# Vision transformer attention: weighted values in two groups a turn, and row maxima of five slots in two halves

## The chip, the cores and the metric

One core of one Trainium2 chip runs the whole program. The metric is the device time of one execution in microseconds (us). The kernel before was run three times: 3645.43, 3633.97 and 3636.25 us, median 3636.25 us.

## The reference

A four-layer vision transformer (64 images, 197 tokens, 8 heads of 16) is followed by a text join, a memory layer and an expert layer. The change lies in the attention of the transformer alone:

```python
for i in range(4):
    y = layernorm(h, ln1_w[i], ln1_b[i])
    q, k, v = split(y @ qkv_w[i] + qkv_b[i])              # 8 heads of 16
    attn = softmax(einsum('bhnd,bhmd->bhnm', q, k) * scale, axis=-1)
    o = einsum('bhnm,bhmd->bhnd', attn, v)                # the weighted values
    h = h + (o @ proj_w[i] + proj_b[i])
    y = gelu(layernorm(h, ln2_w[i], ln2_b[i]) @ fc1_w[i] + fc1_b[i])
    h = h + (y @ fc2_w[i] + fc2_b[i])
```

## The kernel before, in words

Images are taken in pairs, 32 pairs a layer; h lies in SBUF as chunks of 99 tokens. `layers_phase` writes out the order of each engine by hand: each engine has a function `attn(l, i, ...)`, one "turn" for pair i of layer l, that yields three or four times, and `program` calls them in one order on all engines. A turn works on several pairs at once, as a pipeline: LayerNorm statistics of pair i+6, its turning (L449) and K (L491), Q (L457) of i+4 or so, the split of q and k into three bf16 parts for i+4, row maxima of i+1 and i+2, softmax and weighted values of i, projection (L437) of i-2. Turns 0 to 31 of each layer are followed by an MLP stretch, in which the first steps of the next layer's pipeline are dealt out.

**Slots.** A turn has eight slots (`slot(j)`, L418). In each, TensorE (PE) makes four score matmuls of one future unit (`scores`, L346) into the two PSUM banks of `S`, and four transposed score matmuls of one unit of pair i (`scores_t`, L363) into the two banks of `St`. A unit is image b, half of the heads and chunk c; u = 4b + 2 half + c. Slots 0 to 2 take the scores of units 5 to 7 of pair i+1, slots 3 to 7 those of units 0 to 4 of pair i+2. VectorE (DVE) takes the negated row maximum over `S` (`row_max`, L795), one reduction of 788 elements a row; `scores` of the next unit waits for it. ScalarE (ACT) takes exp over `St` into one of four buffers of `probs` (L558); the next `scores_t` waits for it.

**Weighted values.** `pv(l, i, p, b, half)` (L382) multiplies `probs` with `v_aug` in float32: eight matmuls (16 records) on 32 columns each, so that four column strips of the array run side by side, into `O`. One group is run after slots 0, 2 and 6 and ahead of slot 5, so four a turn.

**The maximum's way back.** The row maximum goes into the scores as three more rows of the contraction: when units 0 to 7 of pair i+1 have their maxima, GpSimd (POOL) splits them in three (L687 to L693), PE turns them (L464, into `M2`), DVE copies them (L853), and SyncE (SP) issues three small DMAs into `q_st` (L290). The first `scores_t` of the next turn, called St0 here, waits for them.

**q and k.** PE makes Q (L457) and K (L491) into bank `M0`, ACT adds the bias (L603 for q, L582 for k), POOL makes three bf16 parts of both in four operations (L707, L709, L713, L715), SP writes each part to DRAM (L298) and reads them back, laid out by head, with six DMAs (L305), for the turn after the next but two. SP's queue carries, a turn, in this order: three max rows, six part writes, six reads ("stack loads").

**Other operations named below.** `o_copy` (ACT, L564) takes `O` to SBUF, `o_turn` (PE, L396) turns it into `M1`, `o_norm` (DVE, L803 and L806) divides by the sum, `oT_turn` (PE, L404) and `oT_copy` (ACT, L569) turn it back, the projection (L437) goes into `M0`, and DVE adds it to h (L839), which frees `M0` for Q.

Of the kernel before, what the change touches and what calls it, by code (L numbers as in the profile page):

```python
# [138 lines left out]
NORMED = len(NORM_AT)  # L139


def layers_phase(nc, g, A):

    with ExitStack() as ctx:
# [30 lines left out]
        def places(shapes, at=0):  # L175
# [12 lines left out]
            [(TC, 16 * TB), (128, 2 * PW), (128, 2 * PW), (TC, 4 * D), (TC, 4 * D), (128, PW), (128, PW),  # L188
             (128, PW), (128, PW), (128, PW), (TC, 2 * D)])
        probs, o_n = probs.rearrange("p (u t) -> p u t", u=4), o_n.rearrange("p (c d) -> p c d", d=D)  # L190
# [84 lines left out]
        with nc.Block() as block:  # L275
# [40 lines left out]
            def _(pe):  # L316
# [21 lines left out]
                def scores(l, i, p, even, u):  # L338
# [10 lines left out]
                    mm.then_inc(s["scores"], 1)  # L349
# [18 lines left out]
                def pv(l, i, p, b, half):  # L368
# [10 lines left out]
                    for j in range(4):  # L379
                        for c in range(2):  # L380
# [3 lines left out]
                                                  probs[0:keys, 2 * half + c, j * TB:(j + 1) * TB],  # L384
# [29 lines left out]
                def attn(l, i, p, even, live, y):  # L414
# [12 lines left out]
                    if last:  # L427
                        pv(l, i - 1, p - 1, 1, 1)
# [3 lines left out]
                    if live(-2):  # L432
                        wait(pe, s["oT"], 2 * at(l, i - 1))
                        wait(pe, s["k_f"], at(l, i + 5))
                        peeled(i, ("v_aug", at(l, i + 3)), ("q_f", at(l, i + 4)))
# [5 lines left out]
                    if now:  # L441
                        pv(l, i, p, 0, 0)
                    yield
                    if live(5):
                        wait(pe, s["xn"], at(l, i + 6))
                        wait(pe, s["max_copied"], at(l, i + 1))
                        peeled(i, ("yT", at(l, i + 5)), ("m_yT", y(TURNED_PART)))
# [10 lines left out]
                    slot(4)  # L458
                    yield
                    if nxt:  # L460
                        wait(pe, s["max_split"], 4 * at(l, i + 2))
                        wait(pe, s["yT"], at(l, i + 6))
                        peeled(i, ("max_copied", at(l, i + 1)), ("m_yT", y(MAXED_PART)))
                        nc.tensor.matmul(M2[0:96, 0:TC], max_parts[:].rearrange("p k n -> p (k n)"), ident[:],  # L464
                                         start=True, stop=True).then_inc(s["max_turned"], 1)
                    if now:
                        pv(l, i, p, 0, 1)
                    slot(5)
                    if last:
                        oT_turn(l, i - 1, 1)  # L470
                    if live(3):
                        wait(pe, s["q_f"], at(l, i + 5))
                        peeled(i, ("h_done", at(l, i - 1)), ("k_f", at(l, i + 5)))
                        for t in range(4):
                            mm = nc.tensor.matmul(M0[0:TC, t * D:(t + 1) * D], yT[(p + 3) % 4][:, t * TC:(t + 1) * TC], m.wv,
                                                  start=True, stop=True)
                        mm.then_inc(s["v"], 1)
                    yield
                    slot(6)
                    if now:  # L480
                        pv(l, i, p, 1, 0)
                    slot(7)
                    if now:
                        o_turn(l, i, 0)
                    if live(5):
                        wait(pe, s["yT"], at(l, i + 6))
                        wait(pe, s["v_aug"], at(l, i + 4))
                        peeled(i, ("q_f", at(l, i + 5)), ("k_f", at(l, i + 5)), ("h_done", at(l, i - 1)))
                        if isinstance(i, int) and i < 0:
                            wait(pe, s["w_done"], l + 1)  # L490
                        nc.tensor.matmul(M0[:, 0:PW], m.wk, yT[(p + 1) % 4][:], start=True, stop=True).then_inc(s["k"], 1)  # L491
# [1707 lines left out]
```

## Time and profile before

| | us |
|---|---|
| median of 3 runs | 3636.25 |
| profiled execution | 3640.64 |
| its span (first to last instruction) | 3638.8 |
| PE busy | 3358.6 (92%) |
| PE weight load busy | 2572.5 (71%) |
| DVE busy | 2363.4 (65%) |
| POOL busy | 2263.2 (62%) |
| ACT busy | 2063.2 (57%) |
| mean granted TensorE clock | 0.974 |

Busy time is a sum over the span; matmuls are pipelined, so the difference of two starts, not the length of one, tells what a group of them takes. The attention stretches are four, of about 434 us from the first projection of a layer to its last; some 26 turns of each are steady ones, in which all steps of the pipeline are alive.

### The profile page before, as it was taken

To read this page: it belongs to the slowest core of one execution; us is meant where nothing else is said; L and a number is where in the kernel's file an instruction comes from. 1 tells how busy PE (TensorE), PEld (TensorE's weight loads), DVE (VectorE), ACT (ScalarE), POOL (GpSimd) and SP (SyncE) were. 2 spreads that over 40 slices of the span, in tenths; PEclk is the share of its full clock that TensorE was granted. 3 is DMA by queue.
4 is the path that set the end of the run, shared out by engine and by line. 5 is a ranking of instruction groups with operands and counts; after the bars stand their busy time and mean duration, and the time that the engine had idled before them with its cause. 6 is when DMAs were issued, how large, how long until landed. Compare 5 with 4: busy or idle time off the path is not lost. (4 is left out here: it accounts for less than half of the span.)

```text
span 3638.8 us, 88045 instructions
## 1 busy us (share of the span) xinstructions
PE 3358.6 (92%) x29690; PEld 2572.5 (71%) x29690; DVE 2363.4 (65%) x6342; ACT 2063.2 (57%) x4044; POOL 2263.2 (62%) x2634
## 2 busy tenths in 40 slices
PE   6999999989999898999999999999799898999983
PEld 4577887767777676777777778877544686766762
DVE  2267776657777566777766677766697677885110
ACT  0156666656666665666666566667688464323331
POOL 0356664576666276666638666646697684377886
PEclk9999999999999999999999999999899899999997
DMA  6866665046676315666612666650111233143443
GB/s 218 270 122 126 129 131 102 9 82 125 127 132 127 68 22 100 127 127 131 129 28 55 116 124 130 129 101 2 36 36 28 57 83 58 36 103 73 69 63 32
DMA packets 456075, 342.28 MB, mean 94 GB/s; under 512 B 70659, under 2 KB 440171, under 8 KB 455595
## 3 DMA queue, kind: packets, MB, share of 16 engines
q1 hardware_dynamic: 404419, 275.69, 38.9%
q10 hardware_dynamic: 24224, 46.44, 3.9%
q0 software_dynamic: 27136, 16.42, 3.4%
q8 instruction: 159, 2.61, 0.3%
q14 instruction: 137, 1.12, 0.1%
HBM read 227.68 MB, written 109.29 MB: 93 GB/s over the span
## 5 line engine op out<-in xcount | busy, mean ns | idle before, releaser
L795 DVE TENSOR_REDUCE a_neg_max<-a_S 99x4 f32<-99x788 f32 x1024 | 1003.6, 980 | 487.1 <-PE a_S L346 482.3
L558 ACT ACTIVATE a_shared<-a_St 99x792 f32<-99x792 f32 (+1 forms) x1024 | 851.2, 831 | 636.7 <-PE a_St L363 625.5
L346 PE MATMUL a_S<-a_k_st,a_q_st 96*99 96x197 bf16 x4096 | 538.5, 254 | 40.7 <-DVE a_neg_max L795 40.7
L363 PE MATMUL a_St<-a_q_st,a_k_st 99*99 99x198 bf16 (+1 forms) x4096 | 527.0, 251 | 51.0 <-DMA a_q_st<-a_max_rows 33.9
L346 PEld LDWEIGHTS a_S<-a_k_st,a_q_st 96*99 96x99 bf16 x4096 | 390.1, 126 | 256.3 <-DVE a_neg_max L795 219.1
L382 PE MATMUL a_O<-a_shared,a_v_aug 99*32 99x198 f32 (+1 forms) x8192 | 464.4, 339 | 0.6
L363 PEld LDWEIGHTS a_St<-a_q_st,a_k_st 99*99 99x99 bf16 (+1 forms) x4096 | 389.7, 126 | 80.3 <-DMA a_q_st<-a_max_rows 41.5
L382 PEld LDWEIGHTS a_O<-a_shared,a_v_aug 99*32 99x32 f32 (+1 forms) x8192 | 247.1, 110 | 84.2 <-ACT a_shared L558 1.3
L707 POOL CAST a_parts<-a_q_k 128x792 bf16<-128x792 f32 x128 | 108.1, 844 | 318.0 <-issue 271.7
L687 POOL CAST a_max_parts<-a_neg_max 99x32 bf16<-99x32 f32 x128 | 27.1, 212 | 408.1 <-DVE a_neg_max L795 408.1
L498 PEld LDWEIGHTS a_O<-a_w,a_shared 128*99 128x99 f32 x2048 | 243.3, 167 | 40.4 <-issue 22.6
L498 PE MATMUL a_O<-a_w,a_shared 128*99 128x128 f32 x2048 | 265.9, 274 | 0.9 <-DVE h L892 0.9
L1925 POOL DMA_INDIRECT out<-h,token x128 | 210.2, 1642 | 52.7 <-issue 36.6
L627 ACT ACTIVATE a_shared<-a_St,a_cols 128x396 f32<-128x396 f32 x256 | 148.7, 590 | 149.5 <-PE a_St L509 141.8
L709 POOL TENSOR_TENSOR a_q_k<-a_q_k,a_parts 128x792 f32<-128x792 f32 x128 | 216.3, 1690 | 10.3
L715 POOL TENSOR_TENSOR a_parts<-a_q_k,a_parts 128x792 bf16<-128x792 f32 x128 | 216.0, 1687 | 10.3
L509 PE MATMUL a_St<-a_shared,a_w 128*128 128x396 f32 x512 | 194.3, 502 | 0.0
L723 POOL TENSOR_TENSOR h<-h,a_rows 99x512 f32<-99x512 f32 x128 | 163.1, 1274 | 33.5 <-ACT a_shared L634 33.5
L1869 ACT ACTIVATE z_gel<-z_U,z_sb 128x458 f32<-128x458 f32 x128 | 81.9, 644 | 177.5 <-PE z_U L1747 168.7
L1869 ACT ACTIVATE z_gel<-z_U,z_eb 128x458 f32<-128x458 f32 x128 | 82.4, 644 | 161.7 <-PE z_U L1747 150.0
L1972 DVE TENSOR_TENSOR h<-z_O,xT 120x512 f32<-120x512 f32 x32 | 22.0, 689 | 221.9 <-DMA out<-h,token 172.8
L634 ACT ACTIVATE a_shared<-h,a_m_rstd 99x128 f32<-99x128 f32 x512 | 162.2, 390 | 3.6 <-POOL a_m_rstd L734 3.6
(270 smaller groups left out, 7289.0 us busy)
## 6 DMA issues: line engine op xcount, KB each, us to landing
a_shared<-in_x ACTq DMA_DIRECT2D x64, 594.0 KB, 5.0
spill_q<-a_parts SPq DMA_DIRECT2D x384, 99.0 KB
spill_k<-a_parts SPq DMA_DIRECT2D x384, 99.0 KB
a_k_st<-spill_k SPq DMA_DIRECT2D x128, 297.0 KB, 4.0
a_q_st<-spill_q SPq DMA_DIRECT2D x128, 297.0 KB, 6.2
a_k_st<-spill_k SPq DMA_DIRECT2D x128, 198.0 KB, 4.6
a_q_st<-spill_q SPq DMA_DIRECT2D x128, 198.0 KB, 6.6
a_k_st<-spill_k SPq DMA_DIRECT2D x128, 99.0 KB, 4.8
```

The source lines that it names most:

```text
L346: mm = nc.tensor.matmul(S[0:TC, j // 2, j % 2 * TB:j % 2 * TB + NTOK], q_st[p % 4][0:SPLIT, head, b * TB + c * TC:b * TB + (c + 1) * TC], ...
L363: mm = nc.tensor.matmul(St[0:keys, j // 2, j % 2 * TB:(j % 2 + 1) * TB], k_st[p][:, head, first:first + keys], q_st[p][:, head, b * TB:(b ...
L382: mm = nc.tensor.matmul(O[32 * j:32 * j + 32, half * TB:(half + 1) * TB], v_aug[p % 4][0:keys, 2 * b + c, half * 4 + j, :], probs[0:keys, ...
L498: mm = nc.tensor.matmul(O[0:TC, t * D:(t + 1) * D], gl[k % 2][:, h, t * TC:(t + 1) * TC], m.w2[:, h * D:(h + 1) * D], start=(h == 0), stop ...
L509: nc.tensor.matmul(St[:, h, 0:PW], m.w1[:, h * 128:(h + 1) * 128], m_yT[n % 2], start=True, stop=True).then_inc(s["m_fc1"], 1)
L558: nc.scalar.activation(probs[0:keys, u % 4, :].rearrange("p (x t) -> p x t", x=2), St[0:keys, :, 0:2 * TB], ACT.Exp).then_inc(s["probs"], 1)
L709: nc.gpsimd.tensor_tensor(q_k[:], q_k[:], parts[:, 0, :, :], ALU.subtract).then_inc(s["res"], 1)
L715: nc.gpsimd.tensor_tensor(parts[:, 2, :, :], q_k[:], parts[:, 1, :, :], ALU.subtract).then_inc(s["lo"], 1)
L723: nc.gpsimd.tensor_tensor(hp, hp, m.b2.unsqueeze(1).to_broadcast([TC, 4, D]), ALU.add).then_inc(s["m_bias"], 1)
L795: nc.vector.tensor_reduce(out.rearrange("p (x y) -> p x y", x=2), S[0:TC, :, 0:2 * TB].rearrange("p x (y t) -> p x y t", y=2)[:, :, :, 0:N ...
L1869: nc.scalar.activation(gel[n % 2][:, k, 0:WL], U[k][:, 0:WL], ACT.Gelu_apprx_tanh, bias=bias).then_inc(s["gelu"], 1)
L1925: nc.gpsimd.indirect_dma_start(out=out[:, :], out_offset=bass.IndirectOffsetOnAxis(g.token[0:n, e, k:k + 1].bitcast(U32), 0), in_=y[(2 * e ...
```

## The change

1. PE: `pv` runs as two pairs of groups. Both groups of image 1 of pair i-1 come after slot 0 of the next turn, both groups of image 0 of pair i after slot 4. `probs` gets a fifth buffer, and tables say which unit uses which and what it waits for.
2. DVE: the row maximum of units 0, 2, 3, 4 and 7 is taken in two reductions, one for each bank of `S` (394 elements a row each); the scores of the next unit wait for the halves one by one. Units 1, 5 and 6 stay whole.
3. PE: the turning of the max parts (L464) comes before slot 4 in place of after it, `o_turn` of image 1 before slot 3, V in two parts around slot 6, `o_turn` of image 0 before slot 7, and K goes into `M2`, behind slot 7, and waits for `max_copied`.
4. ACT and DVE: the order of the other operations follows; `oT_copy` of image 0 comes before exp 2, yT before exp 3, the second half of the LayerNorm statistics after the maximum of slot 5.

```diff
+MAX_IN_HALVES = (0, 2, 3, 4, 7)
+PROBS_AT = (3, 0, 1, 4, 2, 0, 1, 4)
+PROBS_FREE = (-3, -1, 0, 0, -1, 1, 2, 2)
 ...  scores
-                    wait(pe, s["row_max"], 8 * at(l, i) + u)
                     for j in range(4):
+                        if j % 2 == 0:
+                            wait(pe, s["row_max"], 16 * at(l, i) + 2 * u - 1 + j // 2)
 ...
+                        if j % 2 == 1:
+                            mm.then_inc(s["scores"], 1)
 ...  attn on PE
                     slot(0)
                     if last:
+                        pv(l, i - 1, p - 1, 1, 0)
                         pv(l, i - 1, p - 1, 1, 1)
                     slot(1)
 ...
                     slot(2)
-                    if now:
-                        pv(l, i, p, 0, 0)
                     yield
 ...
-                    slot(3)
                     if last:
                         o_turn(l, i - 1, 1)
+                    slot(3)
                     if live(4):
                         ...                      # Q
-                    slot(4)
                     yield
                     if nxt:
                         ...                      # turning of the max parts
+                    slot(4)
                     if now:
+                        pv(l, i, p, 0, 0)
                         pv(l, i, p, 0, 1)
                     slot(5)
 ...
-                        for t in range(4):       # V, one part
+                        v(0)
-                    yield
                     slot(6)
-                    if now:
-                        pv(l, i, p, 1, 0)
-                    slot(7)
+                    if live(3):
+                        v(2).then_inc(s["v"], 1)
                     if now:
                         o_turn(l, i, 0)
+                    yield
+                    slot(7)
 ...  K
+                            wait(pe, s["max_copied"], at(l, i + 2))
+                            to = M2
 ...  attn on ACT
-                    wait(act, s["pv"], 4 * at(l, i) + u // 2 - 1)
-                    nc.scalar.activation(probs[0:keys, u % 4, :].rearrange("p (x t) -> p x t", x=2),
+                    wait(act, s["pv"], 4 * at(l, i) + PROBS_FREE[u])
+                    nc.scalar.activation(probs[0:keys, PROBS_AT[u], :].rearrange("p (x t) -> p x t", x=2),
 ...  row_max on DVE
+                    if u in MAX_IN_HALVES:
+                        for x in range(2):
+                            wait(dve, s["scores"], 16 * at(l, i) + 2 * u + x + 1)
+                            nc.vector.tensor_reduce(out[:, x, :], of[:, x], AX.X, ALU.max,
+                                                    negate=True).then_inc(s["row_max"], 1)
+                    else:
+                        wait(dve, s["scores"], 16 * at(l, i) + 2 * u + 2)
+                        nc.vector.tensor_reduce(out, of, AX.X, ALU.max, negate=True).then_inc(s["row_max"], 2)
```

## Rows read from the trace of the kernel before

**Rows 1.** Windows, 24 turns of layer 2: length, busy us, clock, DMA share, GB/s.
```profile
1462.08:1808.28 346.20, 339.39 (x3963) 273.98 (x3961) 257.30 (x521) 233.41 (x384) 224.73 (x286) 1.00 0.69 129
```
**Rows 2.** Timeline of PE, four projections: start us, length us, line, names, count.
```profile
1462.08 1.04 PE L437 MATMUL a_M<-a_w,a_shared 128*99 128x128 f32 x8
...
1808.28 0.93 PE L437 MATMUL a_M<-a_w,a_shared 128*99 128x128 f32 x7
...
477.44 0.82 PE L437 MATMUL a_M<-a_w,a_shared 128*99 128x128 f32 x6
...
491.46 0.71 PE L437 MATMUL a_M<-a_w,a_shared 128*99 128x128 f32 x5
```
**Rows 3.** Page, costliest groups: transposed scores, then idle before them, by releaser.
```profile
L363 PE MATMUL a_St<-a_q_st,a_k_st 99*99 99x198 bf16 (+1 forms) x4096 | 527.0, 251 | 51.0 <-DMA a_q_st<-a_max_rows 33.9
```
**Rows 4.** Timeline of PE in one steady turn, from K to St0 of the next.
```profile
502.32 0.83 PE L491 MATMUL a_M<-a_yT,a_w 128*128 128x396 f32 x2
502.98 0.50 PE L346 MATMUL a_S<-a_k_st,a_q_st 96*99 96x197 bf16 x4
503.63 0.54 PE L363 MATMUL a_St<-a_q_st,a_k_st 99*99 99x198 bf16 x4
504.10 0.90 PE L382 MATMUL a_O<-a_shared,a_v_aug 99*32 99x198 f32 x16
504.93 0.54 PE L346 MATMUL a_S<-a_k_st,a_q_st 96*99 96x197 bf16 x4
...
507.04 0.51 PE L363 MATMUL a_St<-a_q_st,a_k_st 99*99 99x198 bf16 x4
507.47 0.90 PE L382 MATMUL a_O<-a_shared,a_v_aug 99*32 99x198 f32 x16
...
510.83 0.51 PE L363 MATMUL a_St<-a_q_st,a_k_st 99*99 99x198 bf16 x4
511.17 0.21 PE L464 MATMUL a_M<-a_ident,a_max_parts 99*96 99x99 bf16 x1
511.31 0.90 PE L382 MATMUL a_O<-a_shared,a_v_aug 99*32 99x198 f32 x16
...
518.12 0.54 PE L363 MATMUL a_St<-a_q_st,a_k_st 99*99 99x198 bf16 x4 [0.28 <-DMA a_q_st<-a_max_rows]
```
**Rows 5.** Timeline of ACT, same turn: exp of slot 4, then q.
```profile
511.45 0.83 ACT L558 ACTIVATE a_shared<-a_St 99x792 f32<-99x792 f32 x1 [0.65 <-PE a_St L363]
512.18 0.59 ACT L603 ACTIVATE a_q_k<-a_M,a_cols 128x396 f32<-128x396 f32 x1
```
**Rows 6.** Timeline of POOL, same turn: first and last of the max split, last bf16 part.
```profile
508.29 0.21 POOL L687 CAST a_max_parts<-a_neg_max 99x32 bf16<-99x32 f32 x1 [2.10 <-DVE a_neg_max L795]
...
509.18 0.24 POOL L693 TENSOR_TENSOR a_max_parts<-a_max_res,a_max_parts 99x32 bf16<-99x32 f32 x1
...
516.49 1.69 POOL L715 TENSOR_TENSOR a_parts<-a_q_k,a_parts 128x792 bf16<-128x792 f32 x1
```
**Rows 7.** Timeline of SP's queue: stack loads and max rows.
```profile
507.38 1.32 SPq L305 DMA_DIRECT2D a_k_st<-spill_k  x3
508.75 1.44 SPq L305 DMA_DIRECT2D a_q_st<-spill_q  x3
512.83 1.83 SPq L290 DMA_DIRECT2D a_q_st<-a_max_rows  x3
...
521.78 1.32 SPq L305 DMA_DIRECT2D a_k_st<-spill_k  x3
```
**Rows 8.** Windows while the stack loads run: as Rows 1.
```profile
508.50:516.50 8.00, 8.00 (x96) 6.72 (x96) 5.99 (x15) 5.51 (x11) 5.32 (x8) 1.00 1.02 158
```
**Rows 9.** Timeline of DVE, same turn.
```profile
508.13 0.68 DVE L839 TENSOR_TENSOR h<-a_M,h 99x512 f32 x1
...
512.55 0.25 DVE L853 CAST a_max_rows<-a_M 96x99 bf16<-96x99 f32 x1
...
514.45 0.98 DVE L795 TENSOR_REDUCE a_neg_max<-a_S 99x4 f32<-99x788 f32 x1 [0.75 <-PE a_S L346]
515.35 0.37 DVE L863 BATCH_NORM_AGGREGATE a_mv<-a_stats 99x2 f32<-99x6 f32 x4
```

More of the change, by code:

```diff
@@ L383, in pv @@
                                                   v_aug[p % 4][0:keys, 2 * b + c, half * 4 + j, :],
-                                                  probs[0:keys, 2 * half + c, j * TB:(j + 1) * TB],
+                                                  probs[0:keys, PROBS_AT[4 * b + 2 * half + c], j * TB:(j + 1) * TB],
                                                   start=(c == 0), stop=(c == 1))
@@ L445, in attn @@
                         wait(pe, s["xn"], at(l, i + 6))
-                        wait(pe, s["max_copied"], at(l, i + 1))
-                        peeled(i, ("yT", at(l, i + 5)), ("m_yT", y(TURNED_PART)))
+                        wait(pe, s["k_f"], at(l, i + 5))
+                        peeled(i, ("yT", at(l, i + 5)), ("max_copied", at(l, i + 1)), ("m_yT", y(TURNED_PART)))
                         for t in range(4):
@@ L470, in attn, with v @@
                         oT_turn(l, i - 1, 1)
+                    def v(t0):
+                        for t in (t0, t0 + 1):
+                            mm = nc.tensor.matmul(M0[0:TC, t * D:(t + 1) * D], yT[(p + 3) % 4][:, t * TC:(t + 1) * TC], m.wv,
+                                                  start=True, stop=True)
+                        return mm
                     if live(3):
@@ L581, in attn @@
                         wait(act, s["lo"], at(l, i + 4))
-                        nc.scalar.activation(q_k[:, 1, :], M0[:, 0:PW], ACT.Identity, bias=m.bk).then_inc(s["k_f"], 1)
+                        made = M0 if isinstance(i, int) and i <= 0 else M2
+                        nc.scalar.activation(q_k[:, 1, :], made[:, 0:PW], ACT.Identity, bias=m.bk).then_inc(s["k_f"], 1)
+                    if last:
+                        o_copy(l, i - 1, 1)
                     if now:
@@ L589, in attn @@
                     yield
-                    if last:
-                        oT_copy(l, i - 1, p - 1, 0)
-                    if now:
-                        exp(l, i, 3)
                     if live(5):
@@ L598, in attn @@
                     if now:
+                        exp(l, i, 3)
+                    yield
+                    if now:
                         exp(l, i, 4)
-                    yield
                     if live(4):
@@ L604, in attn @@
                     if now:
+                        o_copy(l, i, 0)
                         exp(l, i, 5)
-                        o_copy(l, i, 0)
-                        exp(l, i, 6)
                     if last:
                         oT_copy(l, i - 1, p - 1, 1)
+                    if now:
+                        exp(l, i, 6)
                     yield
@@ L684, in attn @@
                         n, big = at(l, i + 1), neg_max[(p + 1) % 2]
[L685 removed]
+                        wait(pool, s["row_max"], 16 * (n + 1))
                         wait(pool, s["max_turned"], n)
@@ L790, in row_max @@
                     b, half, c = u // 4, u // 2 % 2, u % 2
-                    wait(dve, s["scores"], 8 * at(l, i) + u + 1)
                     if u == 0:
@@ L864, in attn @@
                         op.then_inc(s["aggr"], 1)
-                    if then:
-                        row_max(l, i + 2, p + 2, 4)
                 def mlp(l, k, turned, maxed):
```

37 lines of the change are left out of this document (17 added, 20 removed).

## The prediction

> **What bounds the kernel now.** I read the page first (PE 92% busy), then the windows over 24 steady turns. There PE is busy 339 of 346 us, DVE 257, ACT 233, POOL 225, DMA share 0.69 [rows 1]; first to last projection, this is 346.20 / 24 = 14.42 us a turn [rows 2]. Read no further and PE is the bound. But the turns are not alike: the shortest take 14.02 us (477.44 to 491.46 [rows 2]), others 14.3 to 15.3. Such a 14.02 is PE's own sum; the 0.40 above it is waiting. The page's idle column says for what: of 51.0 us in front of the transposed scores, 33.9 ended with the DMA of the max rows [rows 3]. In the timeline it is St0: its partner in slot 0 starts at 502.98, four such matmuls pass in 0.34 (510.83 to 511.17), so St0 could start at 503.32 and starts at 503.63; in the next turn it starts at 518.12, released by that DMA [rows 4].
>
> Why are the rows late? They are issued at 512.83, over 5 us before St0 [rows 7]; three DMAs of 6 KB do not need that. In between, from 508.5 to 516.5, the 16 DMA engines are full (share 1.02, 158 GB/s) with the six stack loads issued from 507.38 on [rows 7, 8], on the same queue and ahead of them. So the late rows come from the loads, and the loads from a round trip over two turns, which I close by four pieces. St0 at 503.63 to q ready at 512.77 (512.18 + 0.59): 9.14 [rows 4, 5]. From there to the last bf16 part at 518.18: 5.41, all POOL work [rows 6]. From there to the loads' issue at 521.78: 3.60, the writing of the last parts [rows 7]. From loads' issue to St0: 507.38 to 518.12, 10.74 [rows 4, 7]. Sum 28.89 for two turns, 14.45 a turn, beside the measured 14.42. So the steady turn is bounded twice, closely: by this round trip (about 14.4), and by PE (14.02). A change to PE's work alone can give only what it takes out of the round trip.
>
> The Trainium skill's page "DMA: Bandwidth & Descriptors", section "Queues, rings and completion order", says that each DMA engine takes one ring's descriptors in order, but that completion is not first in, first out for an issuing engine, since a small transfer needs only the rings it is on. By the first half the rows must wait as the trace shows; by the second they could slip past, and the round trip would be no bound: that case is the first rival.
>
> **The change part by part.**
>
> *Weighted values in pairs.* The way into a group costs: 0.43 from transposed scores to `pv` (507.04 to 507.47), 0.34 to another group (510.83 to 511.17), so 0.09. A group takes 0.83 (504.10 to 504.93) [rows 4]. Its 16 matmuls, four side by side, would at K's pace (0.66 for two of 396 columns, 502.32 to 502.98 [rows 4], so 0.165 for 198) take 0.66; a second group behind a first costs between 0.66 and 0.83, and I take 0.68. So each merger saves 0.24 (0.09 to 0.26), two a turn 0.49. PE's own sum goes from 14.02 to 13.53.
>
> *Halved maxima.* The trace has no reduction of 394 elements. Bounds: 0.49, half of 0.98, and 0.98. With the copy of 99 elements at 0.25 and the 788 at 0.98 [rows 9] the slope is 1.06 ns an element, so 0.25 + 295 x 1.06 ns = 0.56; I take 0.57. A ready operation starts 0.08 before the end of the one before (515.35 against 515.43 [rows 9]), so a unit costs 1.06 in place of 0.98: +0.08, five a turn, 0.4 us of DVE, which stands idle over 3 us a turn [rows 1]. What it gives: the first half starts after two matmuls, not four (0.17 earlier), and the next unit's first two matmuls wait for the first half alone. That is needed, since slots without `pv` between them now follow at 1.3 to 1.5 us, while scores, maximum, scores took 0.54 + 0.98 + 0.1 = 1.62. Walking the turn slot by slot with these lengths, I find the halves in time everywhere but ahead of slot 6 (0.04); exp leaves St6 0.12 and St0 0.10 late, as its own cycle is 0.54 + 0.83 + 0.1 = 1.47 (exp 0.83 [rows 5]). PE's turn would be 13.8 with the rows in time.
>
> The skill's page "VectorE: DVE Perf Modes", section "The TRN2 errata", speaks against this edit: a fixed cost per instruction makes tiles under 512 elements dear. Its table (120 cycles and one per element at 0.96 GHz for PSUM to SBUF) gives 0.54 us for a half and 0.95 for the whole, where this trace has 0.98; with it the halves cost 0.65 us more a turn before any overlap, still under DVE's idle time.
>
> *Order.* What counts is what lies between St0 and q. Before: St0 to the transposed scores of slot 4 is 7.20 (503.63 to 510.83), and q ends 1.94 later [rows 4, 5]. Both stretches hold two `pv` groups, now merged: -0.24. The turning of the max parts moves in front of slot 4: +0.10 to +0.14 (511.17 to 511.31). Rest unchanged. So St0 to q is 9.14 - 0.12 = 9.02. Three waits are new there. Q waits for the addition to h, queued on DVE behind unit 7's halves: they end 5.09 after St0, the addition (0.68) at 5.68, Q's turn comes at 5.9. The max turning waits for POOL's split, 1.13 long (508.29 to 509.42 [rows 6]): ready at 6.3, wanted at 6.6. Slot 4's second pair of scores waits for unit 0's second half: 6.72, wanted at 6.9. All hold, by 0.2 to 0.3.
>
> *Moved for nothing.* K in `M2` waits for `max_copied`, done (512.80 [rows 9]) 3 us before K. The fifth `probs` buffer keeps exp from waiting for the later `pv`. Max rows are issued about 0.2 earlier than before, but into a queue still full until 516.5 [rows 8]: no gain. Part writes and loads keep their order on SP.
>
> **Sum.** Round trip 28.89 - 0.12, half of it a turn: -0.06. In the turns in which the rows were in time PE can now catch up, up to 14.02 - 13.8; as most turns do wait, I put 0.06 for it. So -0.12 x 26 turns x 4 layers = -12.5 us. The last five turns of a layer load nothing, so no round trip: there PE's gain counts in part, 0.3 (0 to 0.49) x 5 x 4 = -6. Together -18.5: 3640.6 becomes 3622 in this execution's time; it lies 4.4 above the median, so 3618 beside 3636.25. Likeliest case's own range: 3606 to 3628.
>
> **Rivals.**
>
> *The round trip gives way.* If the rows slip past the loads, or the loads end sooner, the turn falls to PE's 13.8 plus some 0.15: -0.47 x 104 = -49, with the ends -55: 3581. For it: PE is busy 98% of the steady window [rows 1]. Against: the full DMA window, and a round trip that sums to the measured turn.
>
> *All is absorbed.* If a second `pv` group costs 0.83 behind a first and the max turning its whole 0.14, St0 to q stays at 9.14 - 0.09 + 0.14; only the ends gain: 3631.
>
> *Slower: q gets late through DVE.* In front of slot 4 there now stand, one behind the other on DVE, two halves of unit 7, the addition, two halves of unit 0. Each 0.1 more in a half puts 0.4 on this chain, less 0.2 of slack, and q with it, half of which goes on every turn. The gain is gone at halves of 0.65, and from 0.69 on the kernel is slower. At 0.78, midway to the upper bound: 4 x 0.21 - 0.18 - 0.12 = 0.54 on the round trip, 0.27 x 104 = +28: 3664. Against: the slope above.
>
> **How the numbers follow.** Forecast 0.45, gives way 0.17, absorbed 0.20, slower 0.18. Under about 0.3% (11 us) no difference can be told here. Of the forecast's 0.45, 0.38 lie beyond it; so faster 0.55, same 0.28, slower 0.17. The range, 3577 to 3646, holds the forecast, the absorbed case, the giving way at its centre, and the mild part of the slower one.
>
> **What would show it.** `pv` in runs of 32 matmuls, 1.5 us to the next group. Halves at 0.57, ten a turn. Idle time before the transposed scores by the max rows' DMA up, from 33.9 towards 60 us or more, DMA share still full before it. St0 to q 9.0. PE's busy time down by some 50 us, the span by less than half of that. Wrong if: the idle time by that DMA falls while the turn shortens (rival one), q comes later than 9.14 after St0 (slower), or a new wait for DVE or exp in front of scores passes 0.4 us a turn.

## The result: slower by 0.8%, and the profile after

The changed kernel takes 3668.85 us (median of five runs, 3659.17 to 3679.85) beside 3636.25, a ratio of 1.0084 [1.0062, 1.0106]. The forecast was 3618 and the range ended at 3646: wrong in sign, and outside the range. The profiled execution took 3679.85, the slowest of the five, its span 3678.1 beside 3638.8 before. So the profiles compared below lie 39.3 us apart, the medians 32.6.

First the page of the changed kernel: the engines' busy time, then the costliest groups (busy us, mean ns of one, idle before and its releaser). The transposed scores are L368 now, they answer to [rows 3].
```profile
PE 3372.0 (92%) x29690; PEld 2620.8 (71%) x29690; DVE 2392.0 (65%) x6982; ACT 2087.4 (57%) x4044; POOL 2258.7 (61%) x2634
...
L814 DVE TENSOR_REDUCE a_neg_max<-a_S 99x2 f32<-99x394 f32 x1280 | 665.5, 563 | 171.1 <-PE a_S L350 158.4
...
L368 PE MATMUL a_St<-a_q_st,a_k_st 99*99 99x198 bf16 (+1 forms) x4096 | 543.6, 256 | 70.0 <-DMA a_q_st<-a_max_rows 45.1
...
L818 DVE TENSOR_REDUCE a_neg_max<-a_S 99x4 f32<-99x788 f32 x384 | 376.4, 980 | 276.7 <-PE a_S L350 276.7
```
The idle time by the max rows' DMA rose from 33.9 to 45.1, as it should if the steady turn is bound by the round trip, though not to the forecast 60. PE's busy time, which was to fall by some 50 us, rose from 3358.6 to 3372.0. A half takes 0.563 us, where 0.57 was taken. Now the steady turn itself, in the timeline of PE, as [rows 4]:
```profile
508.96 0.51 PE L350 MATMUL a_S<-a_k_st,a_q_st 96*99 96x197 bf16 x4
...
510.10 0.54 PE L368 MATMUL a_St<-a_q_st,a_k_st 99*99 99x198 bf16 x4 [0.63 <-DMA a_q_st<-a_max_rows]
510.56 1.59 PE L387 MATMUL a_O<-a_shared,a_v_aug 99*32 99x198 f32 x32
512.08 0.54 PE L350 MATMUL a_S<-a_k_st,a_q_st 96*99 96x197 bf16 x4
...
517.08 0.54 PE L368 MATMUL a_St<-a_q_st,a_k_st 99*99 99x198 bf16 x4
```
A pair of groups costs 1.52 to the next group (510.56 to 512.08; 0.83 + 0.68 = 1.51 was forecast), and St0 to the transposed scores of slot 4 is 6.98 (510.10 to 517.08) in place of 7.20. So the lengths in the steady turn are the forecast ones. The loss is elsewhere, and the windows find it. I cut each execution at the 32 projections of each of the four layers (128 in all): up to the first one; the steady turns (25 a layer); the last turns (projection 26 to 32); from there to the next layer's first (three times); and the rest. The bracket is the time at half the clock, 1.2 GHz in place of 2.4, all in us:

| kernel | first | steady | last turns | between | rest | span |
|---|---|---|---|---|---|---|
| before | 232.3 (0) | 1445.0 (10) | 287.8 (17) | 519.5 (27) | 1154.3 | 3638.8 |
| after | 241.5 (12) | 1433.7 (8) | 314.9 (65) | 530.9 (38) | 1157.0 | 3678.1 |
| difference | +9.2 | -11.2 | +27.2 | +11.4 | +2.7 | +39.3 |

The same in windows of one layer, the third; columns as in [rows 1], the steady turns, the last turns and the way to the next layer. Before:
```profile
1448.06:1808.28 360.22, 353.41 (x4128) 285.39 (x4126) 268.07 (x543) 243.13 (x400) 233.52 (x297) 1.00 0.69 129
1808.28:1877.61 69.33, 61.01 (x722) 46.87 (x721) 41.39 (x91) 44.45 (x74) 16.73 (x31) 1.00 0.29 56
1877.61:2049.47 171.86, 159.35 (x1222) 128.09 (x1220) 114.25 (x401) 101.88 (x233) 129.61 (x153) 0.98 0.30 58
```
After:
```profile
1465.54:1824.00 358.46, 350.42 (x4127) 292.85 (x4126) 273.44 (x668) 248.31 (x400) 232.96 (x297) 1.00 0.69 130
1824.00:1904.41 80.41, 68.71 (x722) 52.67 (x721) 42.36 (x107) 44.85 (x73) 16.69 (x31) 0.89 0.26 48
1904.41:2081.01 176.60, 161.63 (x1221) 131.12 (x1220) 115.00 (x420) 102.63 (x234) 129.45 (x153) 0.97 0.29 57
```
The second line is the finding. The same 722 matmuls with fewer regroupings are *busier* after (68.71 against 61.01), and the mean granted clock is 0.89 where it was 1.00. The two columns belong together: busy time that grows with the same count of instructions is a slower clock, not more work. The page's first lines show none of it: PE at 92% before and after.

### The profile page after: what moved, and what is told of

Its sections match the earlier page's. It is cut to its first block and busy times, and to the rows that moved or that the text cites. A ratio compares the mean times of both kernels' runs of the same rounds, so it can differ in the third digit from the quotient of the medians.

```text
span 3678.1 us, 90295 instructions
## 1 busy us (share of the span) xinstructions
PE 3372.0 (92%) x29690; PEld 2620.8 (71%) x29690; DVE 2392.0 (65%) x6982; ACT 2087.4 (57%) x4044; POOL 2258.7 (61%) x2634
## 5 line engine op out<-in xcount | busy, mean ns | idle before, releaser
L814 DVE TENSOR_REDUCE a_neg_max<-a_S 99x2 f32<-99x394 f32 x1280 | 665.5, 563 | 171.1 <-PE a_S L350 158.4
L368 PE MATMUL a_St<-a_q_st,a_k_st 99*99 99x198 bf16 (+1 forms) x4096 | 543.6, 256 | 70.0 <-DMA a_q_st<-a_max_rows 45.1
L350 PE MATMUL a_S<-a_k_st,a_q_st 96*99 96x197 bf16 x4096 | 548.9, 254 | 44.7 <-DVE a_neg_max L818 29.4
L818 DVE TENSOR_REDUCE a_neg_max<-a_S 99x4 f32<-99x788 f32 x384 | 376.4, 980 | 276.7 <-PE a_S L350 276.7
L368 PEld LDWEIGHTS a_St<-a_q_st,a_k_st 99*99 99x99 bf16 (+1 forms) x4096 | 377.1, 127 | 133.3 <-ACT a_shared L571 66.9
L387 PE MATMUL a_O<-a_shared,a_v_aug 99*32 99x198 f32 (+1 forms) x8192 | 422.2, 344 | 0.0
L387 PEld LDWEIGHTS a_O<-a_shared,a_v_aug 99*32 99x32 f32 (+1 forms) x8192 | 282.8, 112 | 72.0 <-issue 3.5
L577 ACT ACTIVATE a_shared<-a_O 128x396 f32<-128x396 f32 x256 | 128.2, 501 | 101.2 <-PE a_O L387 101.2
```

The lines of the kernel that those rows point to most:

```text
L368: mm = nc.tensor.matmul(St[0:keys, j // 2, j % 2 * TB:(j % 2 + 1) * TB], k_st[p][:, head, first:first + keys], q_st[p][:, head, b * TB:(b ...
L387: mm = nc.tensor.matmul(O[32 * j:32 * j + 32, half * TB:(half + 1) * TB], v_aug[p % 4][0:keys, 2 * b + c, half * 4 + j, :], probs[0:keys, ...
L814: nc.vector.tensor_reduce(out[:, x, :], of[:, x], AX.X, ALU.max, negate=True).then_inc(s["row_max"], 1)
L818: nc.vector.tensor_reduce(out, of, AX.X, ALU.max, negate=True).then_inc(s["row_max"], 2)
```

## What happens in the last turns

Towards the end of a layer the work for later pairs runs out: no Q from turn 28 on, no V from 29, no untransposed scores from slot 3 of turn 30 on. Timeline of PE after, from slot 3 of turn 30 to slot 1 of turn 31 (start, length, idle before it and the releaser):
```profile
1873.72 0.54 PE L368 MATMUL a_St<-a_q_st,a_k_st 99*98 99x198 bf16 x4 [0.48 <-ACT a_shared L571]
1874.63 0.24 PE L466 MATMUL a_M<-a_ident,a_max_parts 99*96 99x99 bf16 x1 [0.36 <-POOL a_max_parts L708]
1875.19 0.54 PE L368 MATMUL a_St<-a_q_st,a_k_st 99*99 99x198 bf16 x4 [0.32 <-ACT a_shared L571]
1875.66 1.59 PE L387 MATMUL a_O<-a_shared,a_v_aug 99*32 99x198 f32 x32
1877.18 0.54 PE L368 MATMUL a_St<-a_q_st,a_k_st 99*98 99x198 bf16 x4
...
1878.64 0.54 PE L368 MATMUL a_St<-a_q_st,a_k_st 99*99 99x198 bf16 x4 [0.75 <-ACT a_shared L571]
...
1880.11 0.54 PE L368 MATMUL a_St<-a_q_st,a_k_st 99*98 99x198 bf16 x4 [0.48 <-ACT a_shared L571]
1881.66 0.87 PE L368 MATMUL a_St<-a_q_st,a_k_st 99*99 99x198 bf16 x4 [1.01 <-ACT a_shared L571]
1882.46 2.89 PE L387 MATMUL a_O<-a_shared,a_v_aug 99*32 99x198 f32 x32
1885.28 0.90 PE L368 MATMUL a_St<-a_q_st,a_k_st 99*98 99x198 bf16 x4
```
And before, from slot 7 of turn 30 to slot 1 of turn 31:
```profile
1858.25 0.54 PE L363 MATMUL a_St<-a_q_st,a_k_st 99*98 99x198 bf16 x4
...
1859.81 0.51 PE L363 MATMUL a_St<-a_q_st,a_k_st 99*99 99x198 bf16 x4 [0.57 <-ACT a_shared L558]
1860.25 0.90 PE L382 MATMUL a_O<-a_shared,a_v_aug 99*32 99x198 f32 x16
1861.59 0.54 PE L363 MATMUL a_St<-a_q_st,a_k_st 99*98 99x198 bf16 x4 [0.44 <-ACT a_shared L558]
```
exp sets the pace here: the slots follow at 1.47 us (1877.18, 1878.64, 1880.11). Before, a weighted group of 0.83 stood in every other slot and filled it. Merged, two stand in one, and PE idles 0.3 to 1.0 us at a time in the others. That alone costs nothing, since exp has the pace. But from 1881.66 on everything takes longer: scores 0.87 for 0.54, and the pair of groups 2.82 (1882.46 to 1885.28) for 1.52. Windows around the two falls of the clock in this layer show what PE did before each; the last row is the same place before the change, where the clock stays up:
```profile
1843.00:1850.80 7.80, 5.75 (x70) 4.57 (x62) 5.82 (x13) 4.22 (x7) 0.00 (x0) 1.00 0.91 133
1850.80:1857.60 6.80, 5.89 (x49) 4.31 (x50) 0.98 (x1) 1.98 (x3) 0.00 (x0) 0.50 0.00 0
...
1871.00:1881.50 10.50, 7.26 (x82) 5.55 (x80) 6.29 (x25) 6.68 (x11) 3.31 (x8) 1.00 0.21 64
1881.50:1888.30 6.80, 6.64 (x52) 5.07 (x53) 0.05 (x1) 3.45 (x9) 1.28 (x1) 0.50 0.00 0
```
```profile
1855.00:1865.00 10.00, 8.01 (x101) 5.61 (x94) 3.42 (x18) 7.54 (x15) 3.67 (x5) 1.00 0.22 67
```
PE was busy 7.26 of 10.50 us, and 5.75 of 7.80; 6.8 us at half the clock followed each. The 5.75 of 7.80 hold idle time of another kind: from 1849.0 on PE waited 2.70 us for the max rows of turn 29, across the fall of the clock, while the DMA share was 0.91 with the last stack loads of the layer, issued in turn 28 (at 1840.67). So idle time that is free by the schedule is paid for by the clock. Over the four layers the time at half the clock rises by 48 us in these turns (17 to 65). Where PE sets the pace, half of that is lost, 24 us, beside the 27.2 measured.

Most of the 27.2 us lies in turns 30 and 31. From projection to projection they take, in this layer, after and then before:
```profile
1871.08:1886.30 15.22, 11.82 (x124) 8.54 (x123) 6.21 (x25) 9.16 (x17) 4.59 (x9) 0.84 0.15 44
1886.30:1900.05 13.75, 11.20 (x115) 8.52 (x114) 3.69 (x14) 7.83 (x15) 1.22 (x2) 0.80 0.01 1
```
```profile
1849.76:1862.14 12.38, 9.91 (x123) 7.15 (x122) 6.16 (x24) 8.93 (x16) 4.56 (x9) 1.00 0.18 54
1862.14:1873.21 11.07, 9.18 (x115) 6.43 (x113) 3.69 (x14) 8.48 (x16) 1.44 (x4) 1.00 0.01 1
```
Over the four layers these two turns take 116.5 us in place of 93.8, so 22.8 of the 27.2.

The Trainium skill's page "TensorE: Matmul & The Clock Gate", section "A second HAM failure mode: psum-queue depth-cycling", says that short idle times between groups of matmuls are enough to swing the clock between its two levels. These rows agree for the second fall: the idle times in front of it are 0.3 to 1.0 us each. They show as well that idle times of that length do not always end so: before, with idle times of 0.44 to 0.75 us at the same place, the clock stays at 2.4 GHz.

## What happens on the way to the next layer

A turn's PE work is handed out by `yield`, and in the last six turns before a layer (the leads) its parts are dealt among the MLP steps. The change put the third `yield` behind slot 6. So the third part holds three slots of untransposed scores (4, 5, 6) in a row, and the fourth part one. In the leads little or nothing lies between the three but the wait for the row maxima. Timeline of PE after, the waits of one such part:
```profile
2027.03 0.54 PE L350 MATMUL a_S<-a_k_st,a_q_st 96*99 96x197 bf16 x4 [1.33 <-DVE a_neg_max L818]
...
2028.71 0.90 PE L350 MATMUL a_S<-a_k_st,a_q_st 96*99 96x197 bf16 x4 [1.14 <-DVE a_neg_max L818]
```
The kernel before has such waits too, but fewer in a row; after, the clock falls behind them (0.90 for 0.54 in the second row). In the first layer the lead ends with St0 waiting for its max rows (after; before it waited 0.33 us):
```profile
236.20 0.88 PE L368 MATMUL a_St<-a_q_st,a_k_st 99*99 99x198 bf16 x4 [2.66 <-DMA a_q_st<-a_max_rows]
```

## The experiments

Fifteen kernels ran. The ratio is to the kernel before on the same chip and carries its 95% interval. The last seven of the table (*) ran on two other chips. There the kernel before takes 3684.1 and 3680.5 us, and in all seven the rest stretch, whose code no edit touches, takes 1193 to 1202 us in place of 1152 to 1157; of these only ratios and stretches are compared. The stretches are those of one profiled execution each.

| kernel | median us | ratio | first | steady | last turns | between |
|---|---|---|---|---|---|---|
| e1_whole_max | 3735.6 | 1.0282 [1.0263, 1.0301] | 241.4 | 1488.3 | 314.9 | 535.6 |
| e2_tail_spread | 3652.1 | 1.0051 [1.0033, 1.0070] | 241.4 | 1438.3 | 294.2 | 523.0 |
| e3_before_split | 3627.8 | 0.9983 [0.9969, 0.9996] | 232.5 | 1435.7 | 280.1 | 516.4 |
| e5_halves_only | 3641.1 | 1.0003 [0.9993, 1.0014] | 234.8 | 1451.6 | 283.7 | 514.7 |
| e6_lead | 3649.7 | 1.0045 [1.0029, 1.0062] | 237.2 | 1433.0 | 315.0 | 517.6 |
| e7_tail_lead | 3642.0 | 1.0001 [0.9989, 1.0012] | 235.4 | 1437.1 | 296.0 | 519.5 |
| e9_before_ring | 3636.7 | 0.9992 [0.9977, 1.0007] | 234.5 | 1434.4 | 290.8 | 520.2 |
| e10_all_ring | 3657.8 | 1.0061 [1.0046, 1.0077] | 234.0 | 1447.7 | 301.1 | 512.9 |
| e8_all* | 3683.2 | 0.9997 [0.9978, 1.0016] | 234.7 | 1442.7 | 301.5 | 514.2 |
| e11_before_light* | 3655.5 | 0.9921 [0.9897, 0.9945] | 234.5 | 1413.2 | 282.7 | 519.6 |
| e12_after_light* | 3680.3 | 0.9987 [0.9968, 1.0007] | 241.0 | 1403.4 | 310.6 | 531.8 |
| e13_filler* | 3706.2 | 1.0059 [1.0040, 1.0079] | 236.1 | 1445.8 | 288.9 | 526.6 |
| e14_lead_filler* | 3676.5 | 0.9986 [0.9970, 1.0001] | 233.2 | 1442.8 | 290.7 | 519.5 |
| e15_before_filler* | 3683.1 | 1.0007 [0.9994, 1.0019] | 232.4 | 1444.1 | 286.6 | 522.6 |
| e16_lead_filler_split* | 3665.2 | 0.9956 [0.9939, 0.9974] | 232.7 | 1423.6 | 291.8 | 516.0 |

One execution says little about a few us: the same code gives different stretches. So read the table by groups. The last turns take 310.6 to 314.9 us in the four kernels with merged groups and no filling (after, e1, e6, e12), 294.2 to 301.5 with the groups one by one again (e2, e7, e8, e10), 288.9 to 291.8 with the filling (e13, e14, e16), and 280.1 to 290.8 in the kernels made from before. The stretches between layers take 523.0 to 535.6 us where the changed kernel has its `yield` behind slot 6, and 512.9 to 519.5 where it is moved back. The steady turns do not part so well: six kernels with the changed kernel's steady turns and order of loads (after, e2, e6, e7, e13, e14) take 1433.0 to 1445.8, before and e15 1445.0 and 1444.1.

**The two halves of the change.** e1 is the change without its halved maxima, e5 the halves without the merging.
```
e1, on after:   MAX_IN_HALVES = ()
e5, on before:  MAX_IN_HALVES = (0, 2, 3, 4, 7)   (and the scores' waits by half)
```


> The changed kernel (3669 us) with every row maximum taken whole again. Theory: the loss is not in the halves but in the ends of the layers and in the steps dealt out among the MLP. Then whole maxima make it worse: ahead of four of the close slots PE waits some 0.15 us more, a steady turn takes about 14.5 in place of 14.35 us, and the time is 3680 to 3695 us. Rival: the ten halves a turn, with their extra waits, cost the 33 us. Then the time falls to 3640 us or below.

> The kernel before (3636 us) with the row maxima of units 0, 2, 3, 4 and 7 in halves, nothing else. Taking the halves out of the changed kernel cost 67 us (3669 to 3736). Theory: that is only so because the pairs of weighted values leave slots next to each other; in the kernel before single groups lie between the slots, PE does not wait for the maximum in its steady turn (14.02 us is its own sum), and the halves change nothing there: 3625 to 3640 us. Rival: the halves are worth some 60 us by themselves, and the pairs cost some 100: then 3570 to 3585 us.


The halves alone do nothing that can be told (e5). With merged groups they are worth some 67 us of the median (3735.6 against 3668.85), 54.6 of it in the steady turns: a larger effect than expected, in the direction expected. Merged groups leave slots with nothing between the scores, and there a whole maximum is PE's wait.

**The last turns.** e2 puts the groups of the last four pairs back one by one.
```
+def paired(i):
+    return not (isinstance(i, int) and i >= 28)
...
-                        pv(l, i, p, 0, 0)
+                        if paired(i):
+                            pv(l, i, p, 0, 0)
...
```


> The changed kernel with the weighted values of pairs 28 to 31 of each layer in four groups a turn again, at the places they had before; all other turns as changed. Theory: where Q, K, V and the scores of later pairs are gone, exp sets the slot at 1.47 us, single groups of weighted values used to fill that time, and pairs of groups stand beside it; the stretch from the 26th to the 32nd projection of a layer falls from 80 to about 72 us (before: 69 to 73), three or four layers, and the time to 3640 to 3652 us. Rival: those stretches are longer because the TensorE clock falls there for another reason, or because of the halves: then they stay near 80 us and the time at 3669 us.


The last turns fall from 314.9 to 294.2, with their time at half the clock from 65 to 20 us. But this mixes two causes, the groups' places and the clock. e13 parts them: it leaves the merged groups where they are and *adds* work. Where a last turn has no Q, V or K, PE multiplies the same operands into a buffer that nobody reads.
```
                     elif now:
                         v(0)
...
                     elif isinstance(i, int) and 28 <= i <= 30:
                         wait(pe, s["max_copied"], at(l, i + 2))
                         nc.tensor.matmul(M2[:, 0:PW], m.wk, yT[(p + 1) % 4][:], start=True, stop=True)
```


> The changed kernel with matmuls in the last turns of each layer (28 to 31) that nobody reads, at the places where Q, V and K stood in the turns before. They fill slots in which PE waits for exp. Theory: the last turns are slow because PE idles there and the granted clock then falls to half; with the filling the clock stays up for most of the time (65 us at half clock in the four stretches of the changed kernel, then 35 us or less), and although PE does some 8 us more work, the four stretches take 296 to 306 us in place of 315, the whole 3652 to 3662 us. Rival: the clock is not what costs there, the longer slots are; then the extra work is added and the time is 3672 us or more.


Windows, sums over the last turns of four layers: after, then e13.
```profile
sum 314.91, PE 273.16 PEld 210.39 DVE 169.50 ACT 179.43 POOL 66.79; mean PE 68.29 PEld 52.60 DVE 42.37 ACT 44.86 POOL 16.70
```
```profile
sum 288.92, PE 270.33 PEld 212.89 DVE 169.40 ACT 179.03 POOL 67.03; mean PE 67.58 PEld 53.22 DVE 42.35 ACT 44.76 POOL 16.76
```
One layer of e13, as the second line of the windows above:
```profile
1207.82:1278.41 70.59, 66.75 (x761) 52.67 (x760) 42.35 (x107) 44.76 (x73) 16.76 (x31) 1.00 0.28 55
```
With some 39 more matmuls in each layer the last turns are shorter by 26.0 us in all, back within 1.2 us of before, and the time at half the clock falls from 65 to 7 us. So the clock makes most of the loss of the last turns; the groups' places matter mainly through it. The median shows less: the ratio falls only from 1.0084 to 1.0059, and the two intervals overlap; in e13's profiled execution the steady turns, whose code is that of the changed kernel, took 12.1 us more. The pair e6 and e14, which differ by the filling alone, shows it clear of noise: 1.0045 [1.0029, 1.0062] and 0.9986 [0.9970, 1.0001].

e15 puts the same filling into the kernel before.

> The kernel before with the same unread matmuls in the last turns of each layer. Theory: there single groups of weighted values fill the slots, only 17 us of these stretches are at half clock, so there is little to win back, and the filling adds PE work to turns of 12.4 and 11.1 us: the four stretches go from 288 us to 290 to 297, the ratio 1.000 to 1.003. Rival: keeping the clock up pays here as well, the four stretches fall to 280 us or less, ratio 0.998 or below.


e15 moves nothing that can be told (last turns 286.6, ratio 1.0007), and is neither the small loss that was forecast for these turns nor the rival's gain. Here the time at half the clock falls too, from 17 to 7 us, but the added work costs as much as that gives.

**The leads.** e6 moves one line, the third `yield`, back in front of slot 6; e7 is e6 and e2 together, e14 is e6 and e13.
```
+                    yield
                     slot(6)
...
-                    yield
```


> The changed kernel with PE's third break of a turn moved from behind slot 6 to ahead of it. It matters only for the first six turns of a layer, whose parts are dealt out one to each step of the MLP before; the order within a turn is unchanged. Theory: part 3 now holds three score slots where it held one, PE waits for row maxima there with nothing else to do, and the stretch from the last projection of a layer to the first of the next takes 177 us in place of 172 to 174. With the break moved it falls by 2 to 4 us a layer, and the time by 8 to 14 us, to 3655 to 3661. Rival: the longer stretch comes from the order inside the turn (K in its own place, V in two parts) or from the clock: then it stays at 177 us.

> The changed kernel with both repairs of the ends: weighted values of pairs 28 to 31 in four groups a turn, and PE's third break ahead of slot 6. Alone they gave 17 and 19 us. Theory: they act in different stretches and add up, 3628 to 3638 us, so about the kernel before. Rival: both act through the same falls of the TensorE clock, so that one takes the gain of the other: 3645 to 3652 us.

> The changed kernel with the order of weighted values left as changed everywhere, PE's third break ahead of slot 6, and the unread matmuls in the last turns of each layer. Theory: the loss of 0.84% is made of the last turns (through the clock) and of the steps dealt out among the MLP (through the break); with both taken away and the steady turn still 0.08 us shorter than before, the last turns take 286 to 292 us in the four layers, the stretches between layers 516 to 521 us in the three, and the time is 0.998 to 1.002 of the kernel before. Rival: a third loss is spread over the kernel that the single profiles do not show: then the ratio stays at 1.004 or above.


Sums from the last projection of a layer to the next one's first: after, then e6.
```profile
sum 530.85, PE 488.79 PEld 394.54 DVE 345.02 ACT 307.41 POOL 388.46; mean PE 162.93 PEld 131.51 DVE 115.01 ACT 102.47 POOL 129.49
```
```profile
sum 517.57, PE 478.47 PEld 387.99 DVE 344.87 ACT 307.96 POOL 388.09; mean PE 159.49 PEld 129.33 DVE 114.96 ACT 102.65 POOL 129.36
```
One line is worth 13.3 us there and 4.3 in the first stretch, a little more than expected. e7 takes both repairs and stands level with before (1.0001): what was lost in the last turns and the leads is the whole loss. It is not the gain hoped for: of the steady turns' -11.2 it keeps 7.9, and its last turns are still 8 us over before. Part of these 8 us can be read from the turns. With the groups one by one and the full clock, turns 30 and 31 take 13.03 and 11.40 us in e7 where before they take 12.38 and 11.06, so 1.0 us a layer is due to the rest of the order, not to the clock; and e7 has 24 us at half the clock in its last turns, before 17. e14 comes out as expected.

**What holds the steady turn: loads, queue or engines?** e11 and e12 load only one head's share into the stacks (the pairs inside the loop score older q and k, so that part is left out). Nothing else changes.
```
+                                heads = HEADS if isinstance(i, int) else 1
+                                sp.dma_start(st[to * HD:(to + n) * HD, 0:heads, :], ...
```


> The kernel before with the six stack loads of the 80 looped turns cut to one head of eight (the scores of these pairs then rest on older q and k; this part of the computation is left out). Every DMA is still issued and waited for, PE, ACT, DVE and POOL do all they did. Theory: the max rows wait for DMA engines that are full with these loads; without them the turn is PE's 14.02 us in all 80 turns, idle time by that DMA under 8 us, the time 3600 to 3606 us. Rival: the rows take their 5 us whatever else is moved: then the time stays above 3625.

> The changed kernel with the same light loads. Theory: the merged groups and halves give PE a turn of 13.88 us in place of 14.02, and that is all that they give where nothing else waits: the steady turn 13.88 and the time 3669 less 80 x 0.47, 3630 to 3636 us; against the light version of before that is -11 us in the loops and +33 and more at the ends. Rival: the PE turn has other waits when the DMA is gone (exp ahead of the transposed scores), and stays at 14.1 or above: 3650 us or more.


Steady turns of one layer, e11 (on before) and then e12 (on after): the DMA share is 0.31 in place of 0.69.
```profile
234.55:586.46 351.91, 351.03 (x4128) 285.43 (x4126) 268.08 (x543) 242.75 (x400) 233.12 (x297) 1.00 0.31 71
```
```profile
1457.81:1806.79 348.98, 347.41 (x4127) 291.30 (x4126) 273.41 (x668) 248.65 (x400) 233.38 (x297) 1.00 0.32 72
```
The records of PE's matmuls now have hardly a gap, and the median turn is 14.02 us in e11 and 13.89 in e12. 14.02 is the one read from the shortest turns of before; e12 saves only 0.13 on it, not the 0.49 of the regroupings. Part of the rest is exp: in these 25 turns of e12 the weight loads of the transposed scores wait 4.8 us for it (21 times), in e11 never. With full loads the median turn is 14.30 before and 14.21 after. So the loads make the wait. (Over the whole of e11 the idle time by the rows' DMA is still 15.9 us, where under 8 was forecast; the unlooped turns keep their full loads.) The same executions show how: a DMA of max rows lands 2.1 us after its issue (median) beside the light loads, and 3.7 us in the changed kernel.

Are they in the way on SP's queue, or at the 16 engines? e9 sends the max rows on ACT's queue; e3 puts the q loads behind the max rows on SP; e10 is e9 with both repairs on after.
```
e9:  -sp.dma_start(...max_rows[part * 32:(part + 1) * 32, :])   (three)
     +act.dma_start(...max_rows[(p + 1) % 2][:])                 (one)
e3:  +if live(3):
     +    stack(i - 1, p - 1, 0)      (q loads of the turn before, behind the max rows)
```


> The kernel before (3636 us) with the max rows in one DMA on ACT's queue (behind o_copy of image 0) in place of three on SP's queue; SP keeps the part writes and the stack loads. So the rows have no loads ahead of them on their queue. Theory: the steady turn of before is set by rows that queue behind the loads; moving half the loads only moved the queue. With a queue of their own the rows are there long before the first transposed scores, idle time by that DMA under 5 us, the steady turn 14.02 to 14.10 us in place of 14.43, and the time 3593 to 3603 us; ACT pays some 0.1 us a turn beside its idle time. Rival: the 16 DMA engines themselves are what the rows wait for, whatever the queue: then the wait stays above 20 us and the time above 3625.

> The kernel before (3636 us) with one change on SP alone: the three loads of q for a pair are issued a turn later, behind the DMAs of the max rows, the three loads of k stay where they are. So the max rows find half the transfer ahead of them. Theory: the steady turn of before is set by the max rows that wait behind the loads; without that it falls from 14.42 to PE's 14.02 us, 104 steady turns, 3590 to 3600 us, and the idle time before the transposed scores by the DMA of the max rows falls from 33.9 us to under 5. Rival: PE's own work is the bound and the wait only stands where another would; then the turn stays at 14.3 to 14.4 and the time at 3630 us or above.

> The changed kernel with both repairs of the ends and the max rows on ACT's queue. Theory: with the round trip out of the way PE's turn decides, 13.89 us (the shortest turn of the changed kernel) in place of 14.35, 104 times, from 3633: 3580 to 3590 us, and some 10 to 15 us under the kernel before with the same queue, which is what the merged groups are worth. Rival: ACT, which has more to do between slots that stand close, loses the issue's time to exp, and the turn stays above 14.1: 3605 us or more.


Timeline of the queues in e9, one turn:
```profile
507.53 1.32 SPq L299 DMA_DIRECT2D a_k_st<-spill_k  x3
508.90 1.44 SPq L299 DMA_DIRECT2D a_q_st<-spill_q  x3
...
513.05 0.73 ACTq L603 DMA_DIRECT2D a_q_st<-a_max_rows  x1
```
And St0 of the next turn, on PE:
```profile
518.09 0.54 PE L357 MATMUL a_St<-a_q_st,a_k_st 99*99 99x198 bf16 x4 [0.44 <-DMA a_q_st<-a_max_rows]
```
The rows have a queue of their own, and St0 still starts 5.04 us after their issue, where it was 5.29 behind the loads (512.83 to 518.12 [rows 4, 7]). The page's idle time by that DMA is 29.8 us in place of 33.9. The forecasts of a gain of some 40 us (e3, e9) and of 50 (e10) missed; e9's rival said that the engines, not the queue, are full, and together with the light loads of e11 the runs bear it out. In e3 the median of 0.9983 is a gain of 6 us and no more. SP then comes to the k loads late, at 6.5 us after the last bf16 part in place of 3.6 (medians), which is the likely reason; no run shows it apart. In e10 the rows are issued 10.0 us after St0, behind ACT's exp, in place of 9.05 in the changed kernel, and the mean steady turn grows to 14.48. e8 (e7 with e3's order) came out level:

> The changed kernel with all three: weighted values of pairs 28 to 31 in four groups, PE's third break ahead of slot 6, and the loads of q behind the max rows on SP's queue. It is the candidate for a version better than both. The first two gave 3642 us together, level with before; moving the loads alone gave the kernel before 0.2%. Theory: with the merged groups PE's floor is 13.88 and the moved loads can give more than they gave before, 3625 to 3635 us. Rival: what holds the turn is the 16 DMA engines, busy with the same bytes in any order: 3636 to 3645 us.

**The version that beats both.** e16 is the change with the lead's `yield` back, the filler, and e3's order of loads.

> As e14_lead_filler, with the loads of q issued behind the max rows. Theory: with the ends repaired and the max rows 0.3 us sooner this is the best version of the change, steady turn 14.25 to 14.35 us, ratio 0.994 to 0.999. Rival: the same bytes keep the DMA engines full in this order too, and the ratio is that of e14_lead_filler within 0.001.


One layer's steady turns in e16:
```profile
2037.92:2393.41 355.49, 348.09 (x4127) 291.32 (x4126) 273.23 (x668) 248.29 (x400) 232.99 (x297) 1.00 0.67 131
```
It takes 0.9956 [0.9939, 0.9974] of the kernel before: 3665.2 beside 3680.5. That is not the worth of the merged groups alone. The same order of loads gave the kernel before 0.9983 [0.9969, 0.9996] on another chip, and e14, without it, is level with before. By these ratios merging, once its side effects are gone, is worth some 0.3%, but the two intervals overlap, so that is not shown.

## Why the prediction was wrong, by its steps

- **The bound of the steady turn: right.** Round trip over the loads, with PE just below it. e11 and e12 show it by making the loads light: the turn falls to 14.02, as read from the shortest turns, and to 13.89.
- **Costs of the parts: right, or nearly.** A second group behind a first 0.69 (0.68 forecast), a half 0.563 (0.57), St0 to q 8.88 (median; 9.02 forecast, 9.13 before, so twice the forecast gain). The steady turns of the profiled pair changed by -11.2 us (the sum's -12.5 was for 104 turns, this is for 100), but by the spread of the other kernels that near hit is in part luck. The halves' need was named, their size not: without them the steady turns lose 55 us. The Trainium skill's page "VectorE: DVE Perf Modes", section "The TRN2 errata", gives its warning for operations that read SBUF; these reductions read PSUM, and by its row for PSUM a half is an estimated 0.54 us and a whole 0.95, where the trace has 0.563 and 0.980.
- **PE's turn of 13.8 with the rows in time: nearly.** e12 gives 13.89. PE's busy time was to fall by some 50 us; in the steady turns it fell by 20 (1419.2 to 1399.4), and over the whole kernel it rose, with 64 us more at half the clock. One sign of being wrong did show: in the steady turns of the changed kernel the weight loads of the transposed scores wait 0.41 us a turn for exp, before not at all.
- **The failed step: "The last five turns of a layer load nothing, so no round trip: there PE's gain counts in part, 0.3 (0 to 0.49) x 5 x 4 = -6."** It came to +27.2. The step had no gain to count, because exp sets the slots there, and it took PE's idle time as free. The clock was at half for 65 us of these turns, 17 before; e13 gave 26.0 back by filling the gaps. Its premise failed too: loads are still issued in turn 28, and St0 of turn 29 waited 2.70 us for its rows in the layer shown, 0.72 before.
- **A step that was missing: the leads.** I walked the loop's turns and not the parts that the leads deal among the MLP steps, where one `yield` decides how many score slots follow each other. The changed kernel takes +11.4 between the layers and +9.2 up to the first projection; e6 gave back 13.3 and 4.3. In e6's first layer St0 still waits 2.00 us for its rows, before 0.33; why was not tried further. Together the two steps make 53.8 of the 57.8 us between the sum's -18.5 and the profiled pair's +39.3.
- **The rivals.** "Slower: q gets late through DVE" had the sign and a near time (3664), but not the cause: q came earlier, so a choice of it would have been right by luck. "The round trip gives way" fell with the 45.1 us of idle time, "all is absorbed" with the -11.2.

What stays open: which part of the order costs e7 the 1.0 us a layer in its last turns, and why e16's steady turns are so short. They take 1423.6 us, while e8, with the same steady turns and the same order of loads, takes 1442.7. e8's have 20.5 us at half the clock and e16's none, which is worth some 10 of the 19; the rest was not tried apart.

## What to carry to other kernels

Price an edit in every stage in which its code runs, the ramp and the drain too: here the pieces of the steady turn came out within 0.02 us, and the loss was in the last 6 of 32 turns and in the leads. Before merging an engine's work, look at where the pieces stand as fillers in another engine's rhythm; idle time in front of a busy PE may be free in the schedule and paid in clock. And when busy time rises while the count of instructions stays, read the granted clock of that window first.

## What the runs showed of the hardware that was not expected

- PE busy 7.26 of 10.50 us was followed by 6.8 us at half the clock (1.2 GHz), in which a pair of groups took 2.82 in place of 1.52 us. Matmuls that nobody reads, in the gaps, made the last turns of the four layers 26.0 us shorter.
- The matmul that waits for a transfer of 18 KB started 5.04 us after the issue with the transfer on a queue of its own, in place of 5.29 on the queue behind six loads. Before, the 16 engines were full until 516.5 (share 1.02, [rows 8]), 1.6 us ahead of that start, and another queue was no way past them. With light loads each third of that transfer landed after 2.1 us, on the same queue as before.
- The same kernel takes 3634 to 3641 us on two chips and 3681 to 3684 on two others. The difference lies behind the last projection: 1154.3 us there before, 1197.8 in e15, whose four layers take within 1.2 us of those of before.
